# Two-layer graph attention on one core: layer 0's LayerNorm passes on VectorE cut from pairs of tiles into single tiles

## The chip, the cores and the metric

The kernel runs on one core of one Trainium2 chip. The metric is the device time of one launch in microseconds (us); lower is better. Everything is in float32.

## The reference, cut to what matters

Eight batches of 2048 nodes with 256 features pass through two layers. Layer 0 is multi-head attention over an adjacency mask, with an output projection, a residual and a LayerNorm with gamma and beta; a second residual and a plain LayerNorm follow. Layer 1 is a graph attention layer; the change doesn't touch it.

```python
# layer 0
q, k, v = x @ Wq.T + bq, x @ Wk.T + bk, x @ Wv.T + bv      # 4 heads of 64
scores = clip(q k^T / 8, -10, 10); scores = where(adj == 0, -10, scores)
ctx = softmax(scores) v
out = ctx @ Wo.T + bo + x
out = (out - mean(out)) * rsqrt(var(out) + 1e-5) * gamma + beta
x1 = layernorm(x + out)
# layer 1
x2 = layernorm(x1 + elu(softmax(mask(leaky_relu(s_i + s_j))) (x1 @ W)))
```

## The kernel before, in words

`layer0` works through the batches one after the other. The queries of a batch are cut into NC = 4 **chunks** of 512, the keys into JB = 16 tiles of 128. One step is one key tile for one chunk; two steps make a **pair** (a "segment" in the code), and a chunk has 8 pairs, numbered k = 0 to 7 here. The work of a pair:

- TensorE (`scores`, L482) makes the scores of one step in two halves (two heads each), so four halves per pair, each 128x1024, in two PSUM buffers (`sc_ps`, one for each half p). Between the halves it does the context and the denominator of an earlier pair (L495, L489) and, in some pairs, one or two projections (q, k, v of this or the next batch, or the output projection "o"). So there are pairs with no projection (`pair_alone`), with one (`pair_with`) and with two (`pair_with_two`). Which pair has which is written in the tables `uses` and `NEXT`. In chunk 0 pairs 0, 1 and 4 have two and the others one; in chunks 1 and 2 pairs 5 to 7 have none, and so has pair 2 of chunk 2; in chunk 3 pairs 0 to 3 have one, pairs 4 to 7 two. Pairs 3 and 4 of each chunk have the output projection of the chunk before. The last batch's chunk 3 has only its output projections.
- VectorE (`clip`, L859) bounds each half: max with -80, min with the mask's bounds; it reads PSUM and the int8 `edges`, and writes `probs`. I call these four instructions the bounds of the pair. After the third of them comes `normalise` (L782), which takes the context of two pairs ago out of PSUM, times the inverted denominator. A scores half can only start when the same half's bound of the step before is done: the third half of a pair waits for its first bound, the fourth for its second, the first half of the next pair for its third, the second half of the next pair for its fourth.
- ScalarE takes the exponential of each half (L383), moves the projections out of PSUM, inverts the denominator (L371, L373), and applies the LayerNorms' scale and offset (`norm`, L364), all in one queue in program order.
- GpSimd (POOL) adds the probabilities of the two steps, once for each half of the heads (`sum_segment`, L280), and adds the segment's context to the chunk's (`add_segment`, L291; nothing to add where k of that segment is 0). Per pair it goes: L280, L291, L280, each on 128x1024 elements in SBUF. The first needs the exponential of the third bound of the pair before. At the end of pairs 3 and 5 it makes the inverse deviations of the LayerNorms on 128x4 numbers.
- SyncE loads the rows of x (`x_rows`) once `s_xfree` says that they are used up, and stores x1 out of `res`.

The LayerNorm of a chunk's 512 rows (T = 4 tiles of 128x256, in `res` and `x_rows`) runs on VectorE between the bounds of the next chunks' scores. Its steps on VectorE:

- `add_bo` (L790): res = x_rows + bo. It waits for the load of `x_rows` and for the store of the old `res`.
- `add_beta` (L796): x_rows = x_rows + beta.
- `add_projection` (L802, L806): res += projection from PSUM, then two `bn_stats` of 128x256.
- `variance` (L815, L817): a tiny memset and four `bn_aggr`.
- `times_gamma` (L822): res = res * gamma, after ScalarE's first norm.
- `add_x` (L829): res = res + x_rows; after the last one `s_xfree` is raised.
- `stats` (L810): `bn_stats` of the second LayerNorm.

`add_bo`, `add_beta`, `times_gamma` and `add_x` each read two operands in SBUF and work on two tiles at once (128x512), two instructions per chunk each: 8 per chunk, 256 in all. All four are `tensor_tensor` and stand at fixed places of `chunk` in the VectorE program, which is an order written out by hand. I name the places by the bound they follow: **place 1** after the first bound of a pair, **place 2** after the second (that is also where `add_projection` stands), **place 4** after the fourth, which is ahead of the next pair's first bound. Nothing but `normalise` stands after the third.

| pair k | before: place 1 | before: place 2 |
|---|---|---|
| 0 | times_gamma (tiles 2, 3) | add_x (0, 1) |
| 1 | add_x (2, 3) | stats 0, 1 |
| 2 | stats 2, 3 | add_bo (0, 1), variance 1 |
| 3 | add_bo (2, 3) | add_projection |
| 4 | | add_projection |
| 5 | variance 0 | add_beta (0, 1) |
| 6 | | add_beta (2, 3) |
| 7 | | times_gamma (0, 1) |

`tail` does the rest of the last two chunks after the last scores.

Of the kernel before, what the change touches and what calls it, by code (L numbers as in the profile page):

```python
# [23 lines left out]
P = 128  # L24
# [11 lines left out]
def layer0(nc, x, xT, adjT, wqT, wkT, wvT, woT, bq, bk, bv, bo, gamma, beta, clip_hi, x1):  # L36
# [37 lines left out]
    def count(b, per, n=0):  # L74
        i, s = b
        return i * (2 * per) + (s * per + n)
# [8 lines left out]
    def back(b, n, per):  # L85
        return (b, n) if n >= 0 else ((b[0], b[1] - 1), n + per)
# [29 lines left out]
    with ExitStack() as ctx:  # L116
# [203 lines left out]
        def _(act):  # L320
# [38 lines left out]
            def norm(b, c, t, which):  # L359
                if t == 0:  # L360
                    act.wait_ge(s_rs[which], count(b, NC, 1 + c + 1))
                    if which == 1:
                        act.wait_ge(s_z, count(b, 2 * NC, 2 * c + 2))
                act.activation(res[:, c % 2, t, :], res[:, c % 2, t, :], ACT.Identity,  # L364
                               scale=rstd[:, which, t:t + 1], bias=nmr[:, which, t:t + 1])\
                   .then_inc(s_n[which], 1)
# [389 lines left out]
        def _(dve):  # L756
# [25 lines left out]
                dve.tensor_tensor(to, ctx_ps[:, :, :], inv_den[:, q % 2, :][:, None, :].broadcast_to([P, HALVES, CW]),  # L782
                                  ALU.mult).then_inc(s_norm, 1)

            def add_bo(b, c, half):
                two = slice(2 * half, 2 * half + 2)
                if half == 0:
                    dve.wait_ge(s_x[c % 2], count(b, 16 * (NC // 2), 16 * (c // 2 + 1)))
                    dve.wait_ge(s_x1[c % 2], count(b, 16 * (NC // 2), 16 * (c // 2 + 1)))
                dve.tensor_tensor(res[:, c % 2, two, :], x_rows[:, c % 2, two, :],  # L790
                                  bo_r[:, None, :].broadcast_to([P, 2, F]), ALU.add).then_inc(s_xb, 1)

            def add_beta(b, c, half):
                two = slice(2 * half, 2 * half + 2)
                dve.wait_ge(s_xb, count(b, 2 * NC, 2 * c + 2))
                dve.tensor_tensor(x_rows[:, c % 2, two, :], x_rows[:, c % 2, two, :],  # L796
                                  beta_r[:, None, :].broadcast_to([P, 2, F]), ALU.add).then_inc(s_xbeta, 1)

            def add_projection(b, c, two, number):
                dve.wait_ge(s_prj, number + 1)  # L800
                dve.wait_ge(s_xb, count(b, 2 * NC, 2 * c + 2))
                dve.tensor_tensor(res[:, c % 2, 2 * two:2 * two + 2, :], prj_ps[:, :].rearrange("p (t f) -> p t f", f=F),  # L802
                                  res[:, c % 2, 2 * two:2 * two + 2, :], ALU.add).then_inc(s_prjfree, 1)
                dve.wait_ge(s_prjfree, 1 + number + 1)
                for t in (2 * two, 2 * two + 1):
                    dve.bn_stats(bn[:, 0, t, :], res[:, c % 2, t, :]).then_inc(s_bn[0], 1)  # L806

            def stats(b, c, t):
                dve.wait_ge(s_z, count(b, 2 * NC, 2 * c + 1 + t // 2))
                dve.bn_stats(bn[:, 1, t, :], res[:, c % 2, t, :]).then_inc(s_bn[1], 1)  # L810

            def variance(b, c, which):
                dve.wait_ge(s_bn[which], count(b, NC * T, T * (c + 1)))
                dve.wait_ge(s_rs[which], count(b, NC, 1 + c))
                dve.memset(tick[:, :], 0.0)  # L815
                for t in range(T):
                    dve.bn_aggr(mv[:, which, t, :], bn[:, which, t, :]).then_inc(s_ag[which], 1)  # L817

            def times_gamma(b, c, half):
                two = slice(2 * half, 2 * half + 2)  # L820
                dve.wait_ge(s_n[0], count(b, NC * T, T * c + 2 * (half + 1)))
                dve.tensor_tensor(res[:, c % 2, two, :], res[:, c % 2, two, :],  # L822
                                  gamma_r[:, None, :].broadcast_to([P, 2, F]), ALU.mult).then_inc(s_gam, 1)

            def add_x(b, c, half):
                two = slice(2 * half, 2 * half + 2)
                dve.wait_ge(s_gam, count(b, 2 * NC, 2 * c + 1 + half))
                dve.wait_ge(s_xbeta, count(b, 2 * NC, 2 * c + 1 + half))
                dve.tensor_tensor(res[:, c % 2, two, :], res[:, c % 2, two, :],  # L829
                                  x_rows[:, c % 2, two, :], ALU.add).then_inc(s_z, 1)  # L830
                if half == 1:
                    dve.wait_ge(s_z, count(b, 2 * NC, 2 * c + 2))
                    dve.sem_inc(s_xfree, 1)

            def clip_piece(i):
# [16 lines left out]
            def clip(b, n, p):  # L852
                c, j = divmod(n, JB)
                pair = slice(2 * p, 2 * p + 2)
                dve.wait_ge(s_fill, count(b, PAIRS * STEPS, PAIRS * n + p + 1))
                if p == 0 and n % SJ == 0:

                    dve.wait_ge(s_pv, count(b, SEGS, n // SJ + 1))
                dve.scalar_tensor_tensor(  # L859
                    out=probs[:, n % RING, pair, :], in0=sc_ps[:, p, :, :], scalar=-LIM,  # L860
                    in1=clip_hi[:, j, c * CW:(c + 1) * CW][:, None, :].broadcast_to([P, 2, CW]),
                    op0=ALU.max, op1=ALU.min).then_inc(s_read, 1)

            def chunk(b, c, prev, more):
                before = back(b, c - 1, NC)
                for k in range(CSEGS):
                    n = c * JB + SJ * k
                    clip(b, n, 0)
                    if prev == 2 and k == 0:
                        times_gamma(*back(b, c - 2, NC), 1)  # L870
                    if prev == 2 and k == 1:
                        add_x(*back(b, c - 2, NC), 1)
                    if prev == 2 and k == 2:
                        stats(*back(b, c - 2, NC), 2)
                        stats(*back(b, c - 2, NC), 3)
                    if prev and k == 3:
                        add_bo(*before, 1)
                    if prev and k == 5:
                        variance(*before, 0)
                    clip(b, n, 1)  # L880
                    if prev == 2 and k == 0:
                        add_x(*back(b, c - 2, NC), 0)
                    if prev == 2 and k == 1:
                        stats(*back(b, c - 2, NC), 0)
                        stats(*back(b, c - 2, NC), 1)
                    if prev and k == 2:
                        add_bo(*before, 0)
                    if prev == 2 and k == 2:
                        variance(*back(b, c - 2, NC), 1)
                    used = use_at(b, n, more)  # L890
                    if used:
                        of, (kind, *which) = used
                        if kind == "o" and prev:
                            add_projection(*before, *which, use_number(b, n, more))
                        if kind == "o" and not prev and which[0] == TO - 1:
                            dve.wait_ge(s_prj, use_number(b, n, more) + 1)
                            dve.sem_inc(s_prjfree, TO)
                    if prev and k in (5, 6):
                        add_beta(*before, k - 5)
                    if prev and k == 7:  # L900
                        times_gamma(*before, 0)
                    clip(b, n + 1, 0)
                    if prev or k >= LAG:
                        normalise(*back(b, n // SJ - LAG, SEGS))
                    clip(b, n + 1, 1)

            def tail(b):
                c = NC - 1
                times_gamma(b, c - 1, 1)
                add_x(b, c - 1, 0)  # L910
                normalise(b, SEGS - LAG)
                add_x(b, c - 1, 1)
                for t in range(T):
                    stats(b, c - 1, t)
                normalise(b, SEGS - 1)
                variance(b, c - 1, 1)
                add_bo(b, c, 0)
                add_bo(b, c, 1)
                for t in range(TO):
                    add_projection(b, c, t, LAST + t)  # L920
                add_beta(b, c, 0)
                add_beta(b, c, 1)
                variance(b, c, 0)
                for half in range(2):
                    times_gamma(b, c, half)
                for half in range(2):
                    add_x(b, c, half)
                for t in range(T):
                    stats(b, c, t)
                variance(b, c, 1)  # L930
# [695 lines left out]
```

## Time and profile before

| | |
|---|---|
| median of 3 runs | 3746.5 us (3744.53 to 3751.67) |
| profiled execution: its time, its span | 3746.31 us, 3744.5 us |
| PE, PE weight loads | 3543.9 us (95%), 2475.5 us (66%) |
| DVE, ACT, POOL | 3105.0 us (83%), 2547.3 us (68%), 2122.0 us (57%) |
| layer 0, layer 1 | about the first 2610 us, the rest |

PE is TensorE's matmul, DVE VectorE, ACT ScalarE, POOL GpSimd. Matmuls are pipelined and their ends are modelled, so a busy PE is not one at its peak. A number behind a name in brackets in the timeline is the idle time of the engine ahead of the instruction, with the instruction that ended it.

### The profile page before, as it was taken

The page shows a single profiled execution, that of the slowest core. Times are in us where ns is not written, and L with a number is a line of the kernel's source. Part 1 is how long each engine was busy: PE and PEld are TensorE (multiplying, and loading weights), DVE is VectorE, ACT ScalarE, POOL GpSimd, SP SyncE. Part 2 cuts the span into 40 slices and gives each one's busy share as a digit, 9 for nine tenths or more (in the row PEclk, how much of TensorE's full clock was granted, in tenths as well). Part 3 has the DMA queues.
Part 4 walks back from the last instruction along what each step waited for, and adds up shares of the span by engine and source line. Part 5 has one row for each costly group of instructions (what it writes and reads, how often), then busy time and mean ns, then how long its engine had stood idle before and what let it go on. Part 6 is the DMA issues. An engine that isn't in the chain of part 4 may idle for free. (4 is left out here: it accounts for less than half of the span.)

```text
span 3744.5 us, 135481 instructions
## 1 busy us (share of the span) xinstructions
PE 3543.9 (95%) x57302; PEld 2475.5 (66%) x57302; DVE 3105.0 (83%) x3575; ACT 2547.3 (68%) x3746; POOL 2122.0 (57%) x1088
## 2 busy tenths in 40 slices
PE   5999999999999999999999999996599999999997
PEld 2656755665675665566567566653478888888886
DVE  6787788688688778868877886896699999999986
ACT  2666666666666666666666666664478889898887
POOL 1787778687678767867877886886011211211120
PEclk9999999999999999999999999998799999999999
DMA  6010010001001000100100100000212121222211
GB/s 230 3 36 14 18 39 14 14 20 39 18 14 36 20 14 15 42 14 14 42 14 14 42 14 14 20 20 27 65 57 69 47 80 58 69 69 69 57 35 57
DMA packets 128570, 145.47 MB, mean 39 GB/s; under 512 B 29777, under 2 KB 113617, under 8 KB 125905
## 3 DMA queue, kind: packets, MB, share of 16 engines
q1 hardware_dynamic: 126704, 136.14, 11.3%
q8 instruction: 474, 7.77, 0.9%
q14 instruction: 144, 1.17, 0.1%
q10 hardware_dynamic: 1248, 0.40, 0.1%
HBM read 102.70 MB, written 33.75 MB: 36 GB/s over the span
## 5 line engine op out<-in xcount | busy, mean ns | idle before, releaser
L280 POOL TENSOR_TENSOR psums<-probs 128x1024 f32<-128x1024 f32 x512 | 1286.9, 2514 | 610.7 <-ACT probs L383 599.4
L383 ACT ACTIVATE probs<-probs 128x1024 f32<-128x1024 f32 x1024 | 1083.8, 1058 | 801.8 <-DVE probs L859 780.0
L495 PE MATMUL ctx_ps<-probs,v_rows 64*32 64x512 f32 x16256 | 1475.4, 590 | 10.0 <-DVE seg_ctx L782 8.9
L859 DVE SCALAR_TENSOR_TENSOR probs<-sc_ps,edges 128x1024 f32<-128x1024 f32 x1024 | 1225.1, 1217 | 197.9 <-PE sc_ps L482 187.4
L482 PE MATMUL sc_ps<-q_cols,k_cols 64*32 64x512 f32 x16384 | 1205.0, 591 | 40.5 <-DVE probs L859 39.8
L1418 PE MATMUL out_ps<-wh,e 128*128 128x257 f32 x4096 | 925.3, 382 | 52.5 <-DVE e L1545 50.5
L1418 PEld LDWEIGHTS out_ps<-wh,e 128*128 128x128 f32 x4096 | 773.5, 191 | 170.1 <-issue 39.0
L495 PEld LDWEIGHTS ctx_ps<-probs,v_rows 64*32 64x32 f32 x16256 | 662.4, 106 | 285.7 <-issue 184.9
L482 PEld LDWEIGHTS sc_ps<-q_cols,k_cols 64*32 64x32 f32 x16384 | 533.0, 107 | 333.0 <-issue 210.1
L489 PE MATMUL den_ps<-psums,ones 64*32 64x512 f32 x4064 | 596.8, 591 | 17.3 <-DVE seg_ctx L782 10.5
L291 POOL TENSOR_TENSOR ctx_t<-ctx_t,seg_ctx 128x1024 f32<-128x1024 f32 x224 | 538.7, 2405 | 50.1 <-DVE seg_ctx L782 50.0
L1242 POOL TENSOR_TENSOR rstd<-var_eps,minus_half 128x4 f32<-128x4 f32 x32 | 109.2, 3412 | 700.6 <-DVE var_eps L1517 700.6
L782 DVE TENSOR_TENSOR seg_ctx<-ctx_ps,inv_den 128x1024 f32<-128x1024 f32 x224 | 274.0, 1223 | 246.3 <-PE ctx_ps L495 196.8
L1300 ACT ACTIVATE e_low<-low,s_fifth 128x512 f32<-128x512 f32 x512 | 363.4, 710 | 35.3 <-DMA low<-rows 29.6
L1303 ACT ACTIVATE e<-high,wh 128x512 f32<-128x512 f32 x512 | 363.3, 709 | 0.0
L1539 DVE TENSOR_TENSOR e<-e,e_low 128x1024 f32<-128x1024 f32 x256 | 318.6, 1245 | 18.5 <-ACT e L1303 14.3
L1473 DVE SCALAR_TENSOR_TENSOR best<-edges,wh,best 128x1024 f32<-128x1024 int8 x240 | 322.7, 1348 | 2.9
L1545 DVE SCALAR_TENSOR_TENSOR e<-edges,e 128x1024 f32<-128x1024 int8 x256 | 311.8, 1218 | 0.0
L489 PEld LDWEIGHTS den_ps<-psums,ones 64*32 64x32 f32 x4064 | 188.7, 106 | 151.8 <-issue 139.8
L516 PE MATMUL prj_ps<-wo,ctx_t 64*32 64x256 f32 x3968 | 265.1, 376 | 0.0
L514 PE MATMUL prj_ps<-wv,x_cols 64*32 64x256 f32 x3904 | 260.7, 378 | 0.0
L509 PE MATMUL prj_ps<-x_cols,wq 64*32 64x256 f32 x3840 | 257.7, 378 | 0.0
(96 smaller groups left out, 3213.4 us busy)
## 6 DMA issues: line engine op xcount, KB each, us to landing
x_cols<-in_xT SPq DMA_DIRECT2D x8, 2048.0 KB, 7.6
probs<-in_adjT SPq DMA_DIRECT2D x16, 1024.0 KB, 8.6
x_rows<-in_x SPq DMA_DIRECT2D x32, 512.0 KB, 4.0
x<-res SPq DMA_DIRECT2D x32, 512.0 KB, 2.9
x_in<-x SPq DMA_DIRECT2D x32, 512.0 KB, 4.6
x_res<-x SPq DMA_DIRECT2D x32, 512.0 KB, 4.9
out<-h SPq DMA_DIRECT2D x32, 512.0 KB, 3.3
high<-rows SPq DMA_DIRECT2D x16, 512.0 KB, 4.2
```

The source lines that it names most:

```text
L280: pool.tensor_tensor(psums[:, q % 2, pair, :], probs[:, (SJ * q) % RING, pair, :], probs[:, (SJ * q + 1) % RING, pair, :], ALU.add).then_i ...
L291: pool.tensor_tensor(ctx_t[:, c % 2, :, :], ctx_t[:, c % 2, :, :], seg_ctx[:, q % 2, :, :], ALU.add).then_inc(s_acc, 1)
L383: act.activation(probs[:, n % RING, pair, :], probs[:, n % RING, pair, :], ACT.Exp, scale=DH ** -0.5).then_inc(s_exp, 1)
L482: last = pe.matmul(sc_ps[quad(g), p, hh, :], k_cols[rows, p, at:at + QUAD], q_cols[rows, c % 2, p, :], start=True, stop=True)
L489: return pe.matmul(den_ps[quad(h), :], ones[head_rows(r), :], psums[head_rows(r), q % 2, h, :], start=(r == 0), stop=(r == 1))
L495: return pe.matmul(ctx_ps[quad(h), z, :], v_rows[head_rows(r), n % JB, at:at + QUAD], probs[head_rows(r), n % RING, h, :], start=start, st ...
L859: dve.scalar_tensor_tensor(out=probs[:, n % RING, pair, :], in0=sc_ps[:, p, :, :], scalar=-LIM, in1=clip_hi[:, j, c * CW:(c + 1) * CW][:, ...
L1300: act.activation(e_low[:, n % LRING, :], low[:, c * CW:(c + 1) * CW], ACT.Exp, bias=s_fifth[:, p, j:j + 1]).then_inc(s_lo, 1)
L1303: act.activation(e[:, n % ERING, :], high[:, c * CW:(c + 1) * CW], ACT.Exp, bias=wh[:, p, j, 1:2]).then_inc(s_hi, 1)
L1418: last = pe.matmul(out_ps[:, bank(c, t), 0:F + 1], e[:, n % ERING, t * P:(t + 1) * P], wh[:, p, j, 3:F + 4], start=(j == 0), stop=(j == JB ...
L1473: dve.scalar_tensor_tensor(out=own, in0=of, scalar=wh[:, p, j, 2:3], in1=own, op0=ALU.min, op1=ALU.max).then_inc(s_best[half], 1)
L1539: dve.tensor_tensor(tiles, tiles, e_low[:, n % LRING:n % LRING + 2, :], ALU.max).then_inc(s_max, 2)
```

## The change

The four pair operations work on one tile of 128x256 each, so 16 in place of 8 per chunk, and every wait on their semaphores counts tiles in place of pairs. They are put at other places, place 4 among them, at most one at each place:

| pair k | after: place 1 | after: place 2 | after: place 4 |
|---|---|---|---|
| 0 | times_gamma 2 | times_gamma 3 | add_x 0 |
| 1 | add_x 1 | add_x 2 | add_x 3 |
| 2 | stats 0, 1 | stats 2, 3, variance 1 | add_bo 2 |
| 3 | add_bo 3 | add_projection | add_beta 0 |
| 4 | add_beta 1 | add_projection | variance 0 |
| 5 | add_beta 2 | add_beta 3 | |
| 6 | | | add_bo 0 (of the running chunk) |
| 7 | add_bo 1 (of the running chunk) | times_gamma 0 | times_gamma 1 |

```diff
@@ ScalarE, norm
-                        act.wait_ge(s_z, count(b, 2 * NC, 2 * c + 2))
+                        act.wait_ge(s_z, count(b, T * NC, T * (c + 1)))
@@ VectorE
-            def add_bo(b, c, half):
-                two = slice(2 * half, 2 * half + 2)
-                if half == 0:
+            def add_bo(b, c, t):
+                if t == 0:
                     dve.wait_ge(s_x[c % 2], count(b, 16 * (NC // 2), 16 * (c // 2 + 1)))
                     dve.wait_ge(s_x1[c % 2], count(b, 16 * (NC // 2), 16 * (c // 2 + 1)))
-                dve.tensor_tensor(res[:, c % 2, two, :], x_rows[:, c % 2, two, :],
-                                  bo_r[:, None, :].broadcast_to([P, 2, F]), ALU.add).then_inc(s_xb, 1)
+                dve.tensor_tensor(res[:, c % 2, t, :], x_rows[:, c % 2, t, :], bo_r[:, :], ALU.add).then_inc(s_xb, 1)
...
-            def times_gamma(b, c, half):
-                two = slice(2 * half, 2 * half + 2)
-                dve.wait_ge(s_n[0], count(b, NC * T, T * c + 2 * (half + 1)))
-                dve.tensor_tensor(res[:, c % 2, two, :], res[:, c % 2, two, :],
-                                  gamma_r[:, None, :].broadcast_to([P, 2, F]), ALU.mult).then_inc(s_gam, 1)
+            def times_gamma(b, c, t):
+                dve.wait_ge(s_n[0], count(b, NC * T, T * c + t + 1))
+                dve.tensor_tensor(res[:, c % 2, t, :], res[:, c % 2, t, :], gamma_r[:, :], ALU.mult).then_inc(s_gam, 1)
...
@@ VectorE, chunk, after the fourth bound of a pair
                     clip(b, n + 1, 1)
+                    if prev == 2 and k == 0:
+                        add_x(*back(b, c - 2, NC), 0)
+                    if prev == 2 and k == 1:
+                        add_x(*back(b, c - 2, NC), 3)
+                    if prev and k == 2:
+                        add_bo(*before, 2)
+                    if prev and k == 3:
+                        add_beta(*before, 0)
+                    if prev and k == 4:
+                        variance(*before, 0)
+                    if k == 6:
+                        add_bo(b, c, 0)
+                    if prev and k == 7:
+                        times_gamma(*before, 1)
```

`add_beta` and `add_x` change in the same way. In the tail each of the pair operations becomes two, four of them (times_gamma 2, 3 and add_x 0, 1) stand ahead of its first `normalise`, and the add_bo of the last chunk's tiles 0 and 1 are gone from it, as they are done in pairs 6 and 7.

## Rows read from the trace of the kernel before

**Rows 1.** Stretch: length, busy PE, PEld, DVE, ACT, POOL, PE clock, DMA, GB/s
```profile
160.00:2580.00 2420.00, 2364.98 (x50200) 1502.02 (x50184) 1959.71 (x2085) 1538.41 (x1888) 1846.20 (x950) 1.00 0.07 22
```

**Rows 2.** Groups of instructions by line, VectorE, same stretch: busy, mean ns, idle before
```profile
L859 DVE SCALAR_TENSOR_TENSOR probs<-sc_ps,edges 128x1024 f32<-128x1024 f32 x982 | 1174.7, 1217 | 167.5 <-PE sc_ps L482 156.9 <-DVE res L829 6.3
...
L796 DVE TENSOR_TENSOR x_rows<-x_rows,beta_r 128x512 f32<-128x512 f32 x62 | 120.9, 1951 | 0.0
...
L790 DVE TENSOR_TENSOR res<-x_rows,bo_r 128x512 f32<-128x512 f32 x61 | 57.6, 945 | 0.0
L806 DVE BATCH_NORM_STATS2 bn<-res 128x6 f32<-128x256 f32 x124 | 46.7, 419 | 2.1
```

**Rows 3.** One line, L796: shortest, median and longest duration
```profile
L796 DVE TENSOR_TENSOR x_rows<-x_rows,beta_r x64: 675/1514/2955, 185.2 to 2599.4; 128x512 f32<-128x512 f32 x64
```

**Rows 4.** Groups of instructions by line, GpSimd, same stretch
```profile
L280 POOL TENSOR_TENSOR psums<-probs 128x1024 f32<-128x1024 f32 x492 | 1239.2, 2519 | 516.3 <-ACT probs L383 505.0 <-DVE ctx_t L782 9.6
L291 POOL TENSOR_TENSOR ctx_t<-ctx_t,seg_ctx 128x1024 f32<-128x1024 f32 x214 | 514.1, 2402 | 48.7 <-DVE seg_ctx L782 48.7
```

**Rows 5.** Timeline of VectorE, pairs 7 and 0 at 1227.72 and 1235.49 us
```profile
1228.40 2.35 DVE L859 SCALAR_TENSOR_TENSOR probs<-sc_ps,edges 128x1024 f32<-128x1024 f32 x2
...
1232.67 0.95 DVE L822 TENSOR_TENSOR res<-res,gamma_r 128x512 f32<-128x512 f32 x1
1233.55 1.21 DVE L859 SCALAR_TENSOR_TENSOR probs<-sc_ps,edges 128x1024 f32<-128x1024 f32 x1
...
1236.17 2.34 DVE L859 SCALAR_TENSOR_TENSOR probs<-sc_ps,edges 128x1024 f32<-128x1024 f32 x2
1238.43 2.86 DVE L822 TENSOR_TENSOR res<-res,gamma_r 128x512 f32<-128x512 f32 x1
1241.21 1.21 DVE L859 SCALAR_TENSOR_TENSOR probs<-sc_ps,edges 128x1024 f32<-128x1024 f32 x1
1242.35 1.74 DVE L829 TENSOR_TENSOR res<-res,x_rows 128x512 f32<-128x512 f32 x1
1244.01 1.21 DVE L859 SCALAR_TENSOR_TENSOR probs<-sc_ps,edges 128x1024 f32<-128x1024 f32 x1
```

**Rows 6.** Timeline of GpSimd, same pairs
```profile
1230.69 2.38 POOL L291 TENSOR_TENSOR ctx_t<-ctx_t,seg_ctx 128x1024 f32<-128x1024 f32 x1
...
1236.02 2.38 POOL L280 TENSOR_TENSOR psums<-probs 128x1024 f32<-128x1024 f32 x1 [0.15 <-ACT probs L383]
1238.36 2.39 POOL L291 TENSOR_TENSOR ctx_t<-ctx_t,seg_ctx 128x1024 f32<-128x1024 f32 x1
1240.70 2.84 POOL L280 TENSOR_TENSOR psums<-probs 128x1024 f32<-128x1024 f32 x1
```

**Rows 7.** Timeline of TensorE, the scores half that starts pair 6
```profile
1219.72 1.09 PE L482 MATMUL sc_ps<-q_cols,k_cols 64*32 64x512 f32 x16 [1.06 <-DVE probs L859]
```

**Rows 8.** Stretches from one pair's first scores to the next's (columns of rows 1)
```profile
1182.01:1191.60 9.59, 8.01 (x152) 3.22 (x152) 7.76 (x14) 6.87 (x9) 7.40 (x3) 1.00 0.48 189
1201.06:1210.51 9.45, 9.45 (x217) 7.15 (x209) 7.38 (x9) 5.85 (x8) 7.09 (x3) 1.00 0.01 3
1210.51:1219.72 9.21, 8.15 (x152) 4.08 (x137) 8.70 (x12) 5.62 (x9) 8.84 (x6) 1.00 0.01 2
1227.72:1235.49 7.77, 7.77 (x152) 3.15 (x144) 6.71 (x7) 6.32 (x9) 7.73 (x4) 1.00 0.02 4
...
1235.49:1245.37 9.88, 9.88 (x217) 6.44 (x201) 9.73 (x7) 5.70 (x8) 7.90 (x4) 1.00 0.01 2
1245.37:1255.27 9.90, 9.90 (x210) 6.03 (x210) 9.27 (x8) 4.95 (x7) 7.52 (x3) 1.00 0.18 54
1255.27:1266.06 10.79, 9.98 (x210) 5.84 (x216) 7.96 (x14) 7.97 (x10) 7.50 (x3) 1.00 0.02 6
```

**Rows 9.** Timeline of ScalarE, the exponential of pair 0's third bound
```profile
1245.49 1.04 ACT L383 ACTIVATE probs<-probs 128x1024 f32<-128x1024 f32 x1
```

**Rows 10.** DMA issues: KB each, median us from issue to landing
```profile
x<-res SPq DMA_DIRECT2D x32, 512.0 KB, 2.9
```

More of the change, by code:

```diff
@@ L783, in normalise, with add_beta @@
                                   ALU.mult).then_inc(s_norm, 1)
-            def add_bo(b, c, half):
-                two = slice(2 * half, 2 * half + 2)
-                if half == 0:
+            def add_bo(b, c, t):
+                if t == 0:
                     dve.wait_ge(s_x[c % 2], count(b, 16 * (NC // 2), 16 * (c // 2 + 1)))
                     dve.wait_ge(s_x1[c % 2], count(b, 16 * (NC // 2), 16 * (c // 2 + 1)))
-                dve.tensor_tensor(res[:, c % 2, two, :], x_rows[:, c % 2, two, :],
-                                  bo_r[:, None, :].broadcast_to([P, 2, F]), ALU.add).then_inc(s_xb, 1)
-            def add_beta(b, c, half):
-                two = slice(2 * half, 2 * half + 2)
-                dve.wait_ge(s_xb, count(b, 2 * NC, 2 * c + 2))
-                dve.tensor_tensor(x_rows[:, c % 2, two, :], x_rows[:, c % 2, two, :],
-                                  beta_r[:, None, :].broadcast_to([P, 2, F]), ALU.add).then_inc(s_xbeta, 1)
+                dve.tensor_tensor(res[:, c % 2, t, :], x_rows[:, c % 2, t, :], bo_r[:, :], ALU.add).then_inc(s_xb, 1)
+            def add_beta(b, c, t):
+                dve.wait_ge(s_xb, count(b, T * NC, T * c + t + 1))
+                dve.tensor_tensor(x_rows[:, c % 2, t, :], x_rows[:, c % 2, t, :], beta_r[:, :], ALU.add)\
+                   .then_inc(s_xbeta, 1)
             def add_projection(b, c, two, number):
                 dve.wait_ge(s_prj, number + 1)
-                dve.wait_ge(s_xb, count(b, 2 * NC, 2 * c + 2))
+                dve.wait_ge(s_xb, count(b, T * NC, T * (c + 1)))
                 dve.tensor_tensor(res[:, c % 2, 2 * two:2 * two + 2, :], prj_ps[:, :].rearrange("p (t f) -> p t f", f=F),
@@ L817, in variance, with add_x @@
                     dve.bn_aggr(mv[:, which, t, :], bn[:, which, t, :]).then_inc(s_ag[which], 1)
-            def times_gamma(b, c, half):
-                two = slice(2 * half, 2 * half + 2)
-                dve.wait_ge(s_n[0], count(b, NC * T, T * c + 2 * (half + 1)))
-                dve.tensor_tensor(res[:, c % 2, two, :], res[:, c % 2, two, :],
-                                  gamma_r[:, None, :].broadcast_to([P, 2, F]), ALU.mult).then_inc(s_gam, 1)
[L825 to L832, printed above, removed]
+            def times_gamma(b, c, t):
+                dve.wait_ge(s_n[0], count(b, NC * T, T * c + t + 1))
+                dve.tensor_tensor(res[:, c % 2, t, :], res[:, c % 2, t, :], gamma_r[:, :], ALU.mult).then_inc(s_gam, 1)
+            def add_x(b, c, t):
+                dve.wait_ge(s_gam, count(b, T * NC, T * c + t + 1))
+                dve.wait_ge(s_xbeta, count(b, T * NC, T * c + t + 1))
+                dve.tensor_tensor(res[:, c % 2, t, :], res[:, c % 2, t, :], x_rows[:, c % 2, t, :], ALU.add)\
+                   .then_inc(s_z, 1)
+                if t == T - 1:
+                    dve.wait_ge(s_z, count(b, T * NC, T * (c + 1)))
                     dve.sem_inc(s_xfree, 1)
@@ L869, in chunk @@
                     if prev == 2 and k == 0:
-                        times_gamma(*back(b, c - 2, NC), 1)
+                        times_gamma(*back(b, c - 2, NC), 2)
                     if prev == 2 and k == 1:
@@ L873, in chunk @@
                     if prev == 2 and k == 2:
+                        stats(*back(b, c - 2, NC), 0)
+                        stats(*back(b, c - 2, NC), 1)
+                    if prev and k == 3:
+                        add_bo(*before, 3)
+                    if prev and k == 4:
+                        add_beta(*before, 1)
+                    if prev and k == 5:
+                        add_beta(*before, 2)
+                    if k == 7:
+                        add_bo(b, c, 1)
+                    clip(b, n, 1)
+                    if prev == 2 and k == 0:
+                        times_gamma(*back(b, c - 2, NC), 3)
+                    if prev == 2 and k == 1:
+                        add_x(*back(b, c - 2, NC), 2)
+                    if prev == 2 and k == 2:
                         stats(*back(b, c - 2, NC), 2)
                         stats(*back(b, c - 2, NC), 3)
[L876 to L888, printed above, removed]
                         variance(*back(b, c - 2, NC), 1)
@@ L897, in chunk @@
                             dve.sem_inc(s_prjfree, TO)
-                    if prev and k in (5, 6):
-                        add_beta(*before, k - 5)
+                    if prev and k == 5:
+                        add_beta(*before, 3)
                     if prev and k == 7:
@@ L905, in chunk @@
                     clip(b, n + 1, 1)
+                    if prev == 2 and k == 0:
+                        add_x(*back(b, c - 2, NC), 0)
+                    if prev == 2 and k == 1:
+                        add_x(*back(b, c - 2, NC), 3)
+                    if prev and k == 2:
+                        add_bo(*before, 2)
+                    if prev and k == 3:
+                        add_beta(*before, 0)
+                    if prev and k == 4:
+                        variance(*before, 0)
[3 more added lines that the diff above has]
+                        times_gamma(*before, 1)
             def tail(b):
                 c = NC - 1
-                times_gamma(b, c - 1, 1)
+                times_gamma(b, c - 1, 2)
+                times_gamma(b, c - 1, 3)
                 add_x(b, c - 1, 0)
+                add_x(b, c - 1, 1)
                 normalise(b, SEGS - LAG)
-                add_x(b, c - 1, 1)
+                add_x(b, c - 1, 2)
+                add_x(b, c - 1, 3)
                 for t in range(T):
@@ L916, in tail @@
                 variance(b, c - 1, 1)
-                add_bo(b, c, 0)
-                add_bo(b, c, 1)
+                add_bo(b, c, 2)
+                add_bo(b, c, 3)
                 for t in range(TO):
                     add_projection(b, c, t, LAST + t)
-                add_beta(b, c, 0)
-                add_beta(b, c, 1)
+                for t in range(T):
+                    add_beta(b, c, t)
                 variance(b, c, 0)
[L924 to L927, printed above, removed]
+                for t in range(T):
+                    times_gamma(b, c, t)
+                for t in range(T):
+                    add_x(b, c, t)
                 for t in range(T):
```

2 lines of the change are left out of this document (1 added, 1 removed).

## The prediction, made before the change was run

> **What bounds the kernel now.** I read the busy times by stretch first. In layer 0's steady part TensorE is busy 2365 of 2420 us, VectorE 1960 and GpSimd 1846 [rows 1]: TensorE sets the pace, and at most a few per cent could come back from it. The lengths of single pairs say where those are [rows 8]. A pair with no projection takes 7.77 us where TensorE never stops, one with an output projection 9.45. The others here are longer than their own kind: 9.21 and 9.59 against 7.77, and 9.88, 9.90 and 10.79 against 9.45. The timeline of TensorE shows what the wait is: pair 6 starts 1.06 us late, and a bound released it [rows 7]. So the bounds are what VectorE owes TensorE, and what stands between them costs time once it exceeds a slack.
>
> What stands between them is dearer than its size. The four pair operations have a shortest time of 0.675 us, a median of 1.51 and a longest of 2.96 for one shape [rows 3], and a mean from 0.95 to 1.95 us by line [rows 2]. Laying the timelines of VectorE and GpSimd side by side gives the reason [rows 5, 6]. The times_gamma of 1232.67 ends at 1233.62; the GpSimd operation under it ended at 1233.07. That of 1238.43 ends at 1241.29, its GpSimd operation at 1240.75. The add_x of 1242.35 ends at 1244.09, GpSimd's at 1243.54. Each time the operation ends 0.54 or 0.55 us behind GpSimd's: **it waits for the running GpSimd operation to end and then runs for 0.55**. GpSimd's next one in turn takes 2.84 in place of 2.39 us, so it waits too. The bounds, with one operand in PSUM, take 1.22 whatever GpSimd does [rows 2].
>
> **What an operation on one tile costs.** After the wait, half of the data. The trace has no such operation. From below: half of 0.55, 0.28. From above: a bn_stats of 128x256, 0.42 [rows 2]. I take 0.28 of record behind GpSimd's end, since it is half of the same instruction, and 0.20 until the next one starts, as a pair's successor starts 0.07 before its end (1241.21 against 1241.29). The wait doesn't shrink with the tile. It is what is left of a 2.38 us operation, from 0 to 2.4, and it's paid once for each instruction: 512 times in place of 256.
>
> The fixed part alone speaks against the change as well. Two singles hold VectorE for up to 2 x 0.42 = 0.84 us against 0.68 [rows 2, 3], so at most 256 x 0.16 = 41 us of VectorE. The Trainium skill (VectorE: DVE Perf Modes, section on the TRN2 errata) has a float32 add at (N+151)/0.96 ns, and advises tiles of 512 elements or more; by it a single is an estimated 424 ns and a pair 691, so 256 x 0.157 = 40 us of VectorE and nothing more, as it counts no wait for GpSimd.
>
> **How long a pair gets.** Between bounds VectorE moves on by 1.14 us (1241.21 to 1242.35) [rows 5]. From these rows the third bound must start 1.37 us before the next pair: 1244.01 against 1245.37 [rows 5, 8]. GpSimd's first operation of the next pair comes 2.39 us behind the third bound at the earliest (one bound, one exponential): that gives it 1.02 us after the pair's start. Now take a pair with a single at places 4, 1 and 2. The place 4 ahead of it is reached at about 1.9 us, in GpSimd's first operation, which ends at 3.40. Single, bound: 3.60 to 4.74. By then GpSimd's second operation runs, from 3.58 to 5.94. Single, bound: 6.14 to 7.28. The third runs to 8.48. Single: third bound at 8.68, next pair at **10.05**. VectorE and GpSimd have gone into step, and each turn costs a whole GpSimd operation. The same walk on the pair before (places 1 and 2 with pairs of tiles, from 1235.49) gives 9.9; it is 9.88 [rows 8].
>
> - Pair 7 with no projection, 17 of them (chunks 1 and 2 of 8 batches, the last chunk 3): three singles in place of one operation. GpSimd starts early there (0.3 to 0.7), since pair 6 has nothing at places 1 and 2. 7.77 becomes 9.4 to 9.7. 17 x 1.7 = +29.
> - Pair 0 with one projection, 22: 9.88 to 10.1, and pair 1, 22: 9.90 to 10.5. With q to take out of PSUM, ScalarE's third exponential ends 5.32 behind the second bound (1246.53 against 1241.21 [rows 5, 9]); with that bound at 6.14 in place of 5.72 it starts GpSimd 1.4 us after the next pair's start, 0.4 later than the third bound alone would. 22 x (0.25 + 0.6) = +18.5. In the last chunk these two have no projection: from 7.77 at best to 10.1, together +4.3.
> - Pair 2: one single is left, at the front; stats and variance don't wait for GpSimd. With a projection, 14: 10.79 to 9.9, as the late start of pair 1 carries over. 14 x -0.9 = -12.6. With none (9.59) it comes out at 9.7: 0.
> - Pair 3, 31: singles at places 4 and 1, then the projection's add and two bn_stats (1.5 us) at 2: third bound near 8.8, 10.15 in place of 9.45. 31 x 0.7 = +21.7.
> - Pair 4 with one projection, 17: the same, +0.7 each, +11.9. Pair 5 with none, 17: two singles that wait at 1 and 2 where one pair did: 9.21 to 9.9. +11.1.
> - Pairs with two projections, and those right behind one: nothing. TensorE is busy over 11 us, and three singles need 10.05. Without that cover each would cost as pair 0. Pair 6: nothing, it only loses work.
> - Tail: four singles ahead of its first normalise, one GpSimd operation each for up to three of them, less the add_bo that are gone. Between -3 and +5; +2.
> - Moved waits: the add_bo of pair 6 waits for a store (2.9 us to land [rows 10]) and a load as large. Both are issued a pair or more earlier, so 0; were one late, VectorE would stand with the next bound behind it. SyncE's load is issued one place 4 later, up to 9 us; its user comes 5 pairs on: 0. `variance` goes from pair 5 to 4, which only helps. ScalarE's queue is untouched.
>
> Sum: 29 + 18.5 + 4.3 - 12.6 + 21.7 + 11.9 + 11.1 + 2 = **+86 us**. Against the profiled execution, 3746.3 (span 3744.5), that is 3832; the median of the runs is 3746.5, the same.
>
> **Rivals.**
> - *Faster: singles find the gaps.* GpSimd is idle for 2420 - 1846 = 574 us, mostly waiting for exponentials [rows 1, 4]. If places 4, 1 and 2 were reached in such gaps, a single would cost 0.34 and the third bound of a pair with one projection be on time. Place: pairs 0, 1, 2 and 5. Price: up to the lengthening that is there now, 0.43, 0.45, 1.34 and 1.44 us a chunk [rows 8], with 22, 22, 22 and 17 pairs: 73 us; half of it gives 3710. It decides where three singles need under 3.8 us in a pair with a projection and 2.1 in one without: a mean record below 1.2 and 0.7. For it: shortest durations of 0.68 exist [rows 3]. Against: after a single GpSimd's next operation starts at once, and VectorE comes back 1.14 us later, inside it.
> - *The wait halves with the tile (sharing in place of waiting).* Then the sum is as before, spread better: 3725 to 3740. The rows speak against it: a constant 0.55 behind three different waits. The Trainium skill (SBUF — State Buffer, on the shared port pair) says that whoever starts first keeps the pair for the whole instruction and the other fully blocks, which excludes this rival; the trace agrees [rows 5, 6].
> - *No difference.* The slack of pairs with projections takes all but pair 7, and pairs 2 and 5 give that back: +29 - 12.6 - 12, within 5 us: 3750.
> - *Slower, but by the fixed part and pair 7 only* (GpSimd not in step at pairs 3, 4, 5): +29 + 18 - 13 = +34: 3780. And the other way: the late start of GpSimd by 0.4 us in every pair of three adds 60 pairs x 0.5: 3860.
>
> **Numbers.** In step as walked 0.60, slower by less (3755 to 3790) 0.20; singles in the gaps 0.09, sharing 0.04; no difference 0.07. What a measurement of this kernel tells from no change is 0.2%, 7.5 us. So faster 0.13, same 0.07, slower 0.80. The range leaves out the faster cases and a little of the rest: 3752 to 3875.
>
> **What would show it.** 512 instructions in the four groups with a mean of 1.1 to 1.5 us, no shortening to half; their sum 560 to 760 us, where some 246 pair instructions at means from 0.95 to 1.95 [rows 2] stood. Pair 7 of chunk 2 near 9.5 us, pair 0 near 10.1, pair 2 of chunk 3 below 10; in each the bounds 3.7 us apart from place to place, and singles ending 0.28 behind GpSimd's end. GpSimd's busy time nearly unchanged, its idle time up; more of TensorE's idle time released by bounds. Wrong would be: a mean below 0.9, or long waits that lie only in pairs with two projections.

## The result and the profile after

The changed kernel takes 3940.2 us (median of 4, 3933.72 to 3945.22) against 3746.8: ratio 1.0513, 95% interval 1.0491 to 1.0535. The forecast was 3832 us, with a range up to 3875: the direction was right, but the loss of 86 us that it gave is less than half of the 193 measured.

Busy times by stretch, the four groups on VectorE, and GpSimd's, after (columns as in [rows 1], [rows 2] and [rows 4]):

```profile
160.00:2770.00 2610.00, 2449.33 (x50216) 1420.30 (x50200) 2231.70 (x2334) 1533.11 (x1891) 1830.49 (x951) 1.00 0.06 21
```

```profile
L793 DVE TENSOR_TENSOR x_rows<-x_rows,beta_r 128x256 f32<-128x256 f32 x128 | 195.0, 1526 | 0.0
L789 DVE TENSOR_TENSOR res<-x_rows,bo_r 128x256 f32<-128x256 f32 x128 | 188.4, 1473 | 0.0
L818 DVE TENSOR_TENSOR res<-res,gamma_r 128x256 f32<-128x256 f32 x128 | 173.5, 1357 | 2.7 <-ACT res L364 2.5
L823 DVE TENSOR_TENSOR res<-res,x_rows 128x256 f32<-128x256 f32 x128 | 168.9, 1323 | 0.0
...
L280 POOL TENSOR_TENSOR psums<-probs 128x1024 f32<-128x1024 f32 x512 | 1248.8, 2440 | 798.8 <-ACT probs L383 790.2 <-DVE seg_ctx L782 7.8
```

Half the data takes nearly as long: 512 instructions with a mean of 1.42 us, 726 us in sum, as forecast (1.1 to 1.5, 560 to 760), where 256 with a mean of 1.58 us, 405 in sum, stood. GpSimd isn't busier, it waits more for ScalarE's exponentials. Before, the same group had

```profile
L280 POOL TENSOR_TENSOR psums<-probs 128x1024 f32<-128x1024 f32 x512 | 1286.9, 2514 | 610.7 <-ACT probs L383 599.4
```

The timelines of VectorE and GpSimd in pairs 7 and 0 of the same batch and chunk as in [rows 5, 6] show the step that the two fall into:

```profile
1308.24 1.21 DVE L853 SCALAR_TENSOR_TENSOR probs<-sc_ps,edges 128x1024 f32<-128x1024 f32 x1
1309.38 1.47 DVE L789 TENSOR_TENSOR res<-x_rows,bo_r 128x256 f32<-128x256 f32 x1
1310.77 1.21 DVE L853 SCALAR_TENSOR_TENSOR probs<-sc_ps,edges 128x1024 f32<-128x1024 f32 x1
1311.91 1.47 DVE L818 TENSOR_TENSOR res<-res,gamma_r 128x256 f32<-128x256 f32 x1
1313.30 1.21 DVE L853 SCALAR_TENSOR_TENSOR probs<-sc_ps,edges 128x1024 f32<-128x1024 f32 x1
```

```profile
1308.00 2.57 POOL L291 TENSOR_TENSOR ctx_t<-ctx_t,seg_ctx 128x1024 f32<-128x1024 f32 x1
1310.53 2.56 POOL L280 TENSOR_TENSOR psums<-probs 128x1024 f32<-128x1024 f32 x1
```

The GpSimd operations end at 1310.57 and 1313.09, the singles at 1310.85 and 1313.38: 0.28 and 0.29 behind. From bound to bound it is 2.53 us. Over the whole trace 456 of the 512 singles end 0.28 or 0.29 us behind a GpSimd operation, and 49 run while none ends and take 0.4 us; before the change 216 of the 256 pair operations ended 0.55 or 0.56 behind one.

The lengths of pairs (as [rows 8]; here chunk 0 pairs 0 and 1 with two projections, then pairs 3, 4, 7 of chunk 2 and 0, 2 of chunk 3; each stretch begins and ends 0.12 us ahead of the first scores, which leaves the lengths as they are):

```profile
1066.34:1080.55 14.21, 12.03 (x286) 7.87 (x279) 9.09 (x8) 6.52 (x8) 7.28 (x4) 1.00 0.01 2
1080.55:1094.87 14.32, 12.03 (x286) 7.82 (x277) 9.11 (x8) 6.61 (x8) 6.95 (x4) 1.00 0.01 3
1267.13:1277.14 10.01, 9.88 (x208) 6.53 (x208) 9.84 (x11) 5.35 (x7) 6.53 (x6) 1.00 0.01 3
1277.14:1287.18 10.04, 9.88 (x208) 6.51 (x208) 10.01 (x11) 5.85 (x7) 7.49 (x3) 1.00 0.01 3
1305.02:1314.54 9.52, 8.25 (x152) 2.70 (x136) 9.52 (x9) 5.83 (x8) 7.67 (x4) 1.00 0.01 2
1314.54:1324.60 10.06, 9.88 (x208) 6.51 (x208) 10.02 (x8) 5.94 (x8) 7.47 (x3) 1.00 0.01 3
1335.09:1345.15 10.06, 9.82 (x208) 5.90 (x216) 8.63 (x15) 5.90 (x7) 7.23 (x3) 1.00 0.18 56
```

Pairs with one projection or none are where the walk put them. The two shown with two projections, which were to cost nothing, stop TensorE for over 2 us each. VectorE, ScalarE and TensorE show why (timelines of the first of these pairs, whose scores start at 1066.46):

```profile
1071.99 1.47 DVE L818 TENSOR_TENSOR res<-res,gamma_r 128x256 f32<-128x256 f32 x1
1073.38 1.21 DVE L853 SCALAR_TENSOR_TENSOR probs<-sc_ps,edges 128x1024 f32<-128x1024 f32 x1
```

```profile
1074.63 1.06 ACT L383 ACTIVATE probs<-probs 128x1024 f32<-128x1024 f32 x1 [1.47 <-DVE probs L853]
1075.59 0.58 ACT L343 ACTIVATE v_rows<-prj_ps 128x512 f32<-128x512 f32 x1
```

```profile
1073.04 1.29 PE L482 MATMUL sc_ps<-q_cols,k_cols 64*32 64x512 f32 x16
1076.36 0.59 PE L495 MATMUL ctx_ps<-probs,v_rows 64*32 64x512 f32 x1 [2.04 <-ACTq L346]
```

The second bound is late (1073.38 to 1074.59), so the second exponential is; behind it in ScalarE's queue stands the copy of the first projection out of PSUM; and the second projection needs that PSUM tile. L346 is the release of the tile. The scores that stand behind it on TensorE, and the context, wait too. TensorE's waits over the whole trace (sum in us, times, longest) show the same release behind copies of v (L346) and k (L334), and once per pair 4 the release by `add_projection` (L799):

```profile
PE ctx_ps L495 <- ACTq L334: 41.4, 20, 2.2
PE ctx_ps L495 <- ACTq L346: 14.3, 7, 2.0
PE ctx_ps L495 <- DVE res L799: 11.4, 14, 0.9
```

**Where the loss is.** I took the length of each of the 255 pairs, from the first scores matmul (L482) of one to that of the next, in both traces, and summed the differences by kind. The two profiled executions are 190 us apart, where the medians are 193:

| pairs | forecast | measured |
|---|---|---|
| two projections (7 or 8 of each place, 52 in all) | 0 | +87 |
| pair 7, none | +29 (with the last chunk's) | +29 |
| pairs 0 and 1, one | +18.5 | +21 |
| pair 2, one and none | -12.6 | -7.5 |
| pair 3, one, all chunks | +21.7 | +31.5 |
| pair 4, one | +11.9 | +10 |
| pair 5, none | +11.1 | +1 |
| other pairs of chunk 0; pair 6 | 0 | +5 |
| last chunk's pairs 0 to 2 | +4.3 | +6 |
| tail and the rest | +2 | +6 |

### The profile page after: what moved, and what is told of

Its sections match the earlier page's. It is cut to its first block and busy times, and to the rows that moved or that the text cites. A ratio compares the mean times of both kernels' runs of the same rounds, so it can differ in the third digit from the quotient of the medians.

```text
span 3934.1 us, 135807 instructions
## 1 busy us (share of the span) xinstructions
PE 3629.4 (92%) x57302; PEld 2392.1 (61%) x57302; DVE 3376.4 (86%) x3831; ACT 2540.7 (65%) x3746; POOL 2109.1 (54%) x1088
## 5 line engine op out<-in xcount | busy, mean ns | idle before, releaser
L280 POOL TENSOR_TENSOR psums<-probs 128x1024 f32<-128x1024 f32 x512 | 1248.8, 2440 | 798.8 <-ACT probs L383 790.2
L482 PE MATMUL sc_ps<-q_cols,k_cols 64*32 64x512 f32 x16384 | 1214.7, 594 | 79.5 <-DVE probs L853 63.4
L495 PEld LDWEIGHTS ctx_ps<-probs,v_rows 64*32 64x32 f32 x16256 | 634.5, 106 | 388.7 <-issue 287.3
L482 PEld LDWEIGHTS sc_ps<-q_cols,k_cols 64*32 64x32 f32 x16384 | 470.7, 106 | 466.0 <-issue 358.8
L291 POOL TENSOR_TENSOR ctx_t<-ctx_t,seg_ctx 128x1024 f32<-128x1024 f32 x224 | 558.8, 2495 | 71.9 <-DVE seg_ctx L782 71.9
L489 PE MATMUL den_ps<-psums,ones 64*32 64x512 f32 x4064 | 578.8, 592 | 18.6 <-DVE seg_ctx L782 7.2
L489 PEld LDWEIGHTS den_ps<-psums,ones 64*32 64x32 f32 x4064 | 175.4, 106 | 170.6 <-issue 161.1
```

What stands on the lines that cost most here:

```text
L280: pool.tensor_tensor(psums[:, q % 2, pair, :], probs[:, (SJ * q) % RING, pair, :], probs[:, (SJ * q + 1) % RING, pair, :], ALU.add).then_i ...
L291: pool.tensor_tensor(ctx_t[:, c % 2, :, :], ctx_t[:, c % 2, :, :], seg_ctx[:, q % 2, :, :], ALU.add).then_inc(s_acc, 1)
L482: last = pe.matmul(sc_ps[quad(g), p, hh, :], k_cols[rows, p, at:at + QUAD], q_cols[rows, c % 2, p, :], start=True, stop=True)
L489: return pe.matmul(den_ps[quad(h), :], ones[head_rows(r), :], psums[head_rows(r), q % 2, h, :], start=(r == 0), stop=(r == 1))
L495: return pe.matmul(ctx_ps[quad(h), z, :], v_rows[head_rows(r), n % JB, at:at + QUAD], probs[head_rows(r), n % RING, h, :], start=start, st ...
```

## The experiments

**No long GpSimd operation to wait for** (e1 with pairs of tiles, e2 with single ones). Segment sums (shown) and context sums (cut in the same way) on 4 elements, `psums` set to 1 once; the denominators and the sum over segments are left out. In both kernels:

```diff
-pool.tensor_tensor(psums[:, q % 2, pair, :], probs[:, (SJ * q) % RING, pair, :],
-                   probs[:, (SJ * q + 1) % RING, pair, :], ALU.add)
+pool.tensor_tensor(psums[:, q % 2, pair, 0:4], probs[:, (SJ * q) % RING, pair, 0:4],
+                   probs[:, (SJ * q + 1) % RING, pair, 0:4], ALU.add)
```

> GpSimd's segment sums cut from 128x1024 to 4 elements per row and head half (denominator and context sums are left out), in the kernel with pairs of tiles. Theory (each of the four operations waits for the running GpSimd operation): the waits vanish, the pair operations record 0.68 us flat, the time falls by 50 to 90 us to 3660 to 3700. Rival (the fixed cost of instructions and their places set the time): the four groups keep a mean above 1 us and the time stays within 20 us of 3747.

> The same cut in the kernel with single tiles at the new places. Theory: singles record 0.40 to 0.42 us and the time comes within 15 us of e1, the loss of 193 us is gone. Rival (256 instructions more and the new places cost in themselves, or ScalarE's queue is what is late in the pairs with two projections): it stays 40 us or more above e1.

3663.3 us with pairs of tiles, 3669.6 with single ones, one run each. One group of each kernel (the other three are the same within 0.01 us):

```profile
L791 DVE TENSOR_TENSOR res<-x_rows,bo_r 128x512 f32<-128x512 f32 x64 | 43.6, 682 | 0.0
```

```profile
L790 DVE TENSOR_TENSOR res<-x_rows,bo_r 128x256 f32<-128x256 f32 x128 | 53.3, 417 | 0.0
```

The 193 us are gone but for 6. So without long GpSimd operations neither 256 more instructions nor the new places cost anything to speak of; the meeting with GpSimd does. It is also worth 83 us in the kernel before (3746.5 to 3663.3), though that counts all that shorter GpSimd operations do. A single is 0.417 us, a pair 0.682, which leaves 0.152 that doesn't shrink with the tile. The formula that the prediction quoted from the Trainium skill (VectorE: DVE Perf Modes, section on the TRN2 errata) gave an estimated 0.424 and 0.691, and these traces agree within 2%. The times hardly show it.

**ScalarE's order in pairs with two projections** (e3).

```diff
+                    if first and second:
+                        take(*first, use_number(b, n, more))
                     exponential(b, n, 1)
-                    if first:
+                    if first and not second:
                         take(*first, use_number(b, n, more))
```

> Single tiles as changed; on ScalarE, in pairs with two projections, the first projection is taken out of PSUM ahead of the second exponential and not behind it. Theory for what the forecast missed: the late second bound delays that exponential, the copy behind it, and so the second projection and everything behind it on TensorE. Then pairs 0 and 1 of chunk 0 and 5 and 7 of chunk 3 go from 14.2 to about 12 us, 60 to 90 us less in all: 3850 to 3880. Rival (TensorE waits there for the third exponential or GpSimd's sum, or for the bound itself): within 15 us of 3940.

3867.1 us (3862.32 to 3870.34), 73 less than the changed kernel. By the same sums over pairs, those with two projections are 15 us above the kernel before, and not 87; all other kinds stay within 2 us of the changed kernel. ScalarE and TensorE in pair 0 of chunk 0, whose scores start at 1041.25:

```profile
1047.85 0.58 ACT L343 ACTIVATE v_rows<-prj_ps 128x512 f32<-128x512 f32 x1
1049.43 1.06 ACT L383 ACTIVATE probs<-probs 128x1024 f32<-128x1024 f32 x1 [1.00 <-DVE probs L855]
```

```profile
1047.83 1.28 PE L484 MATMUL sc_ps<-q_cols,k_cols 64*32 64x512 f32 x16
1048.69 0.59 PE L497 MATMUL ctx_ps<-probs,v_rows 64*32 64x512 f32 x1
```

The bounds are as late as in the changed kernel, and the exponential too (8.18 us into the pair, 8.17 there), but TensorE goes on with no wait. That settles the missing term. Pair 4 keeps 17 us, the others give 2 back: there the first projection is taken by VectorE's `add_projection` and not by ScalarE, and TensorE still waits for it 14 times, 11.5 us in all.

**Single tiles, old places** (e4). Each pair operation becomes two singles, one behind the other:

```diff
                     if prev == 2 and k == 0:
-                        times_gamma(*back(b, c - 2, NC), 1)
+                        times_gamma(*back(b, c - 2, NC), 2)
+                        times_gamma(*back(b, c - 2, NC), 3)
```

> Each pair operation is cut into two single ones, both at the place the pair had; nothing at the fourth place. Theory (one wait per instruction, GpSimd goes between two singles): 512 waits, the second single of two lasts up to 2.6 us where GpSimd has work, mean above 1.2 us, 3820 to 3960. Rival A (VectorE runs the second single before GpSimd's next operation): mean of the second 0.4, within 15 us of 3747, and the new places are what costs. Rival B (fixed cost only): 3750 to 3790 with a mean of 0.4 to 0.9.

3964.3 us (3959.47 to 3964.56), just over the upper end of the expectation, and mean durations from 1.32 to 1.56. VectorE and GpSimd in pair 0 of chunk 2:

```profile
1251.91 3.06 DVE L818 TENSOR_TENSOR res<-res,gamma_r 128x256 f32<-128x256 f32 x2
```

```profile
1249.77 2.38 POOL L280 TENSOR_TENSOR psums<-probs 128x1024 f32<-128x1024 f32 x1 [2.59 <-ACT probs L383]
...
1252.12 2.56 POOL L291 TENSOR_TENSOR ctx_t<-ctx_t,seg_ctx 128x1024 f32<-128x1024 f32 x1
```

Two singles with nothing of VectorE's between them take 3.06 us: GpSimd's L291 gets its turn between them, and the second ends at 1254.97, 0.29 behind GpSimd's 1254.68. The places are those of the kernel before, the count of instructions is not, and 218 us are lost. So the count is what costs; the new places are, if anything, 24 us better.

**The other way: four tiles at once** (e5; e6 and e7 add e3's order to it and to the kernel before). One operation is shown; all four change so, and with them the places, as the expectation says.

```diff
-                dve.tensor_tensor(res[:, c % 2, two, :], res[:, c % 2, two, :],
-                                  gamma_r[:, None, :].broadcast_to([P, 2, F]), ALU.mult)
+                dve.tensor_tensor(res[:, c % 2, :, :], res[:, c % 2, :, :],
+                                  gamma_r[:, None, :].broadcast_to([P, T, F]), ALU.mult)
```

> The other way: each of the four operations takes all four tiles at once (128x1024), 4 waits per chunk in place of 8, all at the first place (times_gamma in pair 0, add_x in 1, add_bo in 3, add_beta in 5; variance 0 behind the second bound of pair 5). Theory (a wait per instruction, then its length): 128 instructions of 1.1 us behind GpSimd's end, mean 1.5 to 3.4 us; pairs 0 and 1 with one projection 9.45 us, pair 2 near 9.5, pair 5 with none near 8.5; pairs with two projections up to 0.7 longer. In all 40 to 65 us less than before: 3682 to 3706. Rival (what counts is how long one stall lasts, since up to 3.4 us stand between two bounds): slower than before, 3760 or more.

> e5 with ScalarE's first projection of two taken ahead of the second exponential, as in e3. Theory: the pairs with two projections lose their 0.6 us waits, 8 to 20 us less than e5: 3665 to 3695. Rival (with the second bound near time the order on ScalarE doesn't matter): within 5 us of e5.

> The kernel with pairs of tiles, with only ScalarE's order changed as in e3. Theory: the second bound is seldom late in pairs with two projections there, so only pair 1 of chunk 0 gains (12.4 to 11.8 us): 3 to 8 us less, 3737 to 3743. Rival (the order is worth the 73 us of e3 in any kernel): under 3700.

e5 took 3798.9 us, ratio 1.0138 (1.0122 to 1.0153): a miss, and the rival's outcome. e6 gave 3777.1 (1.0083, 1.0069 to 1.0097): 22 us less than e5, a little over the 8 to 20 expected, but 82 above its expected span, as e5 is 93 above its own. e7 gave 3740.8 (0.9985, 0.9976 to 0.9994), as expected. In e5 pair 0 is 9.45 us as the theory had it, but pair 1 is 10.74 and pair 2 10.22. VectorE and ScalarE in pair 1 of chunk 2, whose scores start at 1191.10:

```profile
1192.47 1.22 DVE L782 TENSOR_TENSOR seg_ctx<-ctx_ps,inv_den 128x1024 f32<-128x1024 f32 x1 [2.23 <-ACT inv_den L373]
1193.61 2.35 DVE L853 SCALAR_TENSOR_TENSOR probs<-sc_ps,edges 128x1024 f32<-128x1024 f32 x2
1195.87 3.21 DVE L824 TENSOR_TENSOR res<-res,x_rows 128x1024 f32<-128x1024 f32 x1
1199.32 2.36 DVE L853 SCALAR_TENSOR_TENSOR probs<-sc_ps,edges 128x1024 f32<-128x1024 f32 x2 [0.23 <-DVE res L824]
1203.83 1.22 DVE L782 TENSOR_TENSOR seg_ctx<-ctx_ps,inv_den 128x1024 f32<-128x1024 f32 x1 [2.15 <-ACT inv_den L373]
```

```profile
1200.57 1.06 ACT L383 ACTIVATE probs<-probs 128x1024 f32<-128x1024 f32 x1 [3.53 <-DVE probs L853]
1201.54 0.67 ACT L337 ACTIVATE q_cols<-prj_ps,bq_c 128x512 f32<-128x512 f32 x1
1202.38 0.60 ACT L371 ACTIVATE inv_den<-den_ps 128x512 f32<-128x512 f32 x1 [0.17 <-ACT q_cols L337]
1203.01 0.63 ACT L373 ACTIVATE inv_den<-inv_den 128x512 f32<-128x512 f32 x1
```

It is the same chain as in the pairs with two projections, one link further: late second bound, exponential, copy, the two steps of the inversion, and then normalise. The normalise at 1192.47 is pair 0's, 2.23 us late; VectorE's fourth bound of pair 0 and the bounds of pair 1 stand behind it, so that pair 1's second bound comes 8.2 us after its start. The normalise at 1203.83 does the same to pair 2, 2.15 us late. TensorE waits for normalise as well (from the waits of e5; 10.5 us, 6 times in the kernel before):

```profile
PE den_ps L489 <- DVE seg_ctx L782: 37.2, 27, 2.4
```

That was a reading of rows until the next three runs.

**ScalarE's queue in other pairs** (e8 with four tiles, e9 with two, e10 with one). In chosen pairs the copy and the inversion go ahead of the second exponential; shown for e8 and e9, while e10 does it in all pairs but 6. The two are moved together, so that the runs don't tell what each is worth:

```diff
+                    ahead = prev and k in (0, 1, 5)
+                    if first and (second or ahead):
+                        take(*first, use_number(b, n, more))
+                    if ahead:
+                        invert(*back(b, n // SJ - LAG, SEGS))
                     exponential(b, n, 1)
...
-                    if prev or k >= LAG:
+                    if not ahead and (prev or k >= LAG):
                         invert(*back(b, n // SJ - LAG, SEGS))
```

> e6, and in pairs 0, 1 and 5 ScalarE takes the projection out of PSUM and inverts the denominator ahead of the second exponential. Theory (a late second bound costs through ScalarE's in-order queue: exponential, projection, inversion, then normalise and the next pair): normalise comes on time, pair 1 goes from 10.7 to 9.5, pair 2 from 11.4 to 9.5 (with a projection) and 10.2 to 8 (without), 60 to 95 us less than e6: 3680 to 3715. Rival (GpSimd's late third sum, or the stall of 3.4 us itself, lengthens those pairs): within 20 us of e6.

> e7 (pairs of tiles), with ScalarE's order in pairs 0, 1 and 5 as in e8. Theory: pair 2 falls from 10.8 to 9.5 with a projection and from 9.6 to 8.0 without, pairs 0 and 1 stay near 9.8 as their third bound is late by itself: 20 to 40 us less than e7, 3700 to 3720. Rival: within 8 us of e7.

> e3 (single tiles as changed), with ScalarE's order as in e8 in all pairs but 6. Theory: what ScalarE's queue added goes (pairs 1 and 3 from 10.5 to 10.05, pairs 2 and 6 of chunk 0), what the steps of VectorE and GpSimd cost stays: 3830 to 3855, still 80 us or more above the kernel before. Rival (the queue was the whole loss): 3770 or less.

| tiles per instruction | ScalarE as before | copy first, two projections | copy and inversion first |
|---|---|---|---|
| four | 3798.9 | 3777.1 | 3690.8 |
| two | 3746.5 | 3740.8 | 3709.3 |
| one | 3940.2 | 3867.1 | 3825.5 |

All three fell: by 86, 31 and 42 us against the column before (e10 to 4.5 us below the expected span). In the run of e8, pairs 0, 1 and 2 of chunk 2 (each stretch begins and ends 0.3 us behind the first scores), and the second and third bounds and normalise of pair 1 on VectorE:

```profile
1137.16:1146.61 9.45, 9.45 (x216) 6.84 (x208) 8.98 (x7) 6.54 (x9) 8.05 (x3) 1.00 0.02 3
1146.61:1156.07 9.46, 9.46 (x219) 7.13 (x211) 8.98 (x7) 5.94 (x8) 8.07 (x3) 1.00 0.26 94
1156.07:1164.48 8.41, 8.15 (x155) 3.90 (x147) 8.04 (x15) 5.49 (x7) 7.30 (x4) 1.00 0.53 211
```

```profile
1152.78 2.36 DVE L858 SCALAR_TENSOR_TENSOR probs<-sc_ps,edges 128x1024 f32<-128x1024 f32 x2 [0.24 <-DVE res L829]
1155.38 1.22 DVE L787 TENSOR_TENSOR seg_ctx<-ctx_ps,inv_den 128x1024 f32<-128x1024 f32 x1 [0.25 <-PE ctx_ps L500]
```

`add_x` holds VectorE as long as in e5 (3.21 us), but the second bound comes 6.5 us into pair 1 and not 8.2, normalise waits for TensorE alone, and TensorE doesn't stop in pairs 0 and 1. So the long stall cost e5 its time mostly by ScalarE's queue, and not by its length. With the queue out of the way fewer, longer instructions are the better choice, as the theory said: **e8 takes 3690.8 us, ratio 0.9856 (0.9838 to 0.9873), 1.4% less than the kernel before, and beats both kernels.** With single tiles 79 us above the kernel before are left in e10, and 116 above e9. By the sums over pairs the largest parts of the 79 are 29 us in pair 7, 17 in pair 3, 10 in pair 4 with one projection, 11 in pairs 0 and 1 with one, where VectorE's and GpSimd's turns are as before, and 17 in pair 4 with two.

## Why the prediction was right, and where it was wrong

- *A wait for GpSimd per instruction, whatever the tile's size*: right. 0.28 and 0.29 us behind GpSimd's end where 0.28 was taken; e1, e2 and e4 show it as cause. The sharing rival and, but for five pairs, the one of gaps found no place: no mean below 1.32.
- *How long a pair gets*: right for pairs of one projection or none. 10.05 was worked out for three singles, 10.06 measured; 9.4 to 9.7 against 9.52 for pair 7 of chunk 2; 10.15 against 10.01 and 10.04 for pairs 3 and 4 of chunk 2. These terms gave 84 us together, and 96 were measured; single ones were off by up to 10. Pair 3 in chunks 0, 1 and 3 takes 10.5 to 10.9 us, which e10's order on ScalarE takes back to at most 10.14, so a late normalise was behind it. Pair 5's term counted 17 pairs, but five of them (chunk 1 of the first batch, chunk 2 of the last but one, and the three of the last) take 7.99 us in place of some 9.27, as their singles find GpSimd in a gap: there the gap rival was right. That the sum came near is in part luck, as pair 3 missed by +10 and pair 5 by -10.
- *"In each the bounds 3.7 us apart from place to place"*, among the signs, doesn't follow from the walk, which has bounds at 3.60 and 6.14, so 2.54 apart; 2.53 was measured. Pair 2 of chunk 3, to be below 10 us, took 10.06.
- *"Pairs with two projections, and those right behind one: nothing. TensorE is busy over 11 us, and three singles need 10.05"*: this is the step that failed. Three singles do fit before the pair's end: its third bound at 1074.85 comes 8.4 us after the start. But I compared only the bounds with the scores that need them. I left out who else is queued behind the second bound: ScalarE's exponential, its copy, and so the second projection in the middle of the pair. Measured 14.21 and 14.32 us, where the same pairs took 11.94 and 12.38 from first scores to first scores before, +87 us over all pairs of this kind (but none of it in chunk 3's pair 6, which has no single at places 1 and 2: 11.82 against 11.78). e3 takes 72 of them away by the order of two operations on ScalarE, and leaves 17 in pair 4, where TensorE waits for `add_projection` (11.5 us of them; no run tests it). Of the 104 us by which the traces exceed the forecast (190 against 86) this term is 87. Why pair 1 of chunk 0 and pair 7 of chunk 3 take 16.0 us in five cases, and not 14.3, stays open; e3 takes that back too.
- The prediction had read that queue for one pair (pair 1, the 5.32 us of [rows 9]) and sized its effect on GpSimd, and didn't ask the same for the others. "ScalarE's queue is untouched" was true of its order, not of its lateness. e7 and e9 show that it was worth 37 us already in the kernel before, 6 by the copy and 31 by copy and inversion.
- The fixed part: at most 41 us of VectorE, of which e2 against e1, a single run each, leaves 6 in the time.

## What to carry to other kernels

Where VectorE operations with two SBUF operands run beside long GpSimd operations, count the instructions, not the elements: here each could wait for a whole GpSimd operation (1.42 us on average for 0.42 of work). So few and long ones are better, or places that GpSimd is known to leave free. But a long one holds up what stands behind it longer: four tiles at once lost 52 us until ScalarE's queue was reordered, and were the best choice after. When an instruction is made late, follow every in-order queue that it feeds, not only the engine that sets the pace: the dearest waiter here was TensorE's second projection, behind a copy that stood behind the late exponential, in a pair that had 2 us to spare by its bounds. And check whether such a queue can be reordered: in the kernel before that alone gave 37 us, and only then did going from two tiles to four give another 19.

## What the runs showed that was not expected

Two VectorE operations in a row, with GpSimd waiting, don't run in a row: GpSimd's operation of 2.38 us comes between them (e4: 3.06 us for two of 0.42). Wherever in e4 a GpSimd operation stood ready as the first of two singles ended, 156 times, the second ended 0.28 or 0.29 us behind it. And VectorE in turn came first again when that one ended, though GpSimd's next was ready: 2.57 and 2.56 us in its records in place of 2.38. The two take turns. Which of the two comes first can hang on little: in pair 5 with no projection GpSimd's first operation starts 1.02 us after the pair in 12 cases and 1.09 in five. In the 12 its second operation starts some 0.07 us ahead of the single at 3.45, which then takes 2.6 us and the pair 9.84. In the five both start within 0.01 us of 3.44, the single comes first and takes 0.41, GpSimd's record grows to some 2.67, and the pair takes 7.99.
